# Causal attention stage: per-group helper work moved from ScalarE to VectorE, one multiply folded away, and two look-aheads deepened by one

## The reference

```python
qkv = einsum('bse,fe->bsf', ln(x), w_in)            # 32 query heads, 8 K/V heads, D = 128
q, k = apply_rope(q), apply_rope(k)
scores = einsum('bqhgd,bkhd->bhgqk', q, k) / sqrt(128), causal mask
out = einsum('bhgqk,bkhd->bqhgd', softmax(scores), v)
x = x + ln(einsum('bse,fe->bsf', out, w_out))
xf = ln(x)
routing = softmax(xf @ gate_w.T)                     # 8 experts
y = (xf * (routing @ in_scale)) @ sign(weight).T * (routing @ out_scale) + bias
x = x + ln(y)
```

## Time and profile before

| what | us |
|---|---|
| two timed runs | 9707.69, 9943.1 (median 9825.4) |
| profiled execution, its time | 9640.5 |
| its span on the slowest core (core 4) | 9639.0 |
| spans of all cores | 9559.4 to 9639.0 |
| attention in it (about 2451 to 5883) | 3432 |
| mean granted TensorE clock, all cores | 0.675 to 0.679 |

### The profile page before, as it was taken

How to read it: one execution, slowest core, us unless ns; L and a number is a source line. 1 busy time by engine, 2 the same in 40 slices (tenths; PEclk the granted TensorE clock), 3 DMA queues, 4 the chain that set the end, 5 groups by cost and what they waited for, 6 DMA issues and landing times.

```text
span 9639.0 us, 67201 instructions; the slowest of 8 cores (9559.4 to 9639.0 us)
## 1 busy us (share of the span) xinstructions
PE 6412.1 (67%) x22496; PEld 2183.9 (23%) x22496; DVE 1823.5 (19%) x1540; ACT 1753.5 (18%) x2929; POOL 248.5 (3%) x283
## 2 busy tenths in 40 slices
PE   1277777786567778888888886888831157988400
PEld 1133333333111111111111111333310023333100
DVE  3211111111232111111111110000034450000244
ACT  2200000001333232222222220000012211111111
POOL 0011111100000000000000000000000000000000
PEclk7688888898555555555555555799965569999755
DMA  2221122222100000000000003112122222121233
GB/s 89 72 40 36 37 40 40 40 45 65 42 10 24 6 6 22 5 4 5 4 4 4 4 4 97 41 43 51 46 93 109 109 69 50 34 50 45 78 140 139
DMA packets 118321, 442.99 MB, mean 46 GB/s; under 512 B 13665, under 2 KB 87521, under 8 KB 88033
## 3 DMA queue, kind: packets, MB, share of 16 engines
q0 software_dynamic: 16912, 119.74, 6.9%
q10 hardware_dynamic: 12962, 176.18, 4.7%
q1 hardware_dynamic: 88128, 142.78, 4.1%
HBM read 415.78 MB, written 142.61 MB: 58 GB/s over the span
## 4 chain that ended last, share of the span: by engine, by line
PE 65%; DMA 12%; DVE 12%; ACT 5%; issue 3%; another core or an unknown queue 1%; POOL 1%; ACTq 0%; DVEq 0%; POOLq 0%; SPq 0%
PE PA L544 6%; PE PA L358 5%; PE PB L358 5%; DVE recT_sb L605 4%; DMA wq_sb<-wqkv 4%; PE PB L562 3%; PE PB L572 3%; PE PA L691 3%; PE PB L691 3%; PE PF L537 3%; PE PE L537 3%; PE PB L853 3%; PE PA L853 3%; DVE stats L228 3%; DMA x_t<-xin 3%
## 5 line engine op out<-in xcount | busy, mean ns | idle before, releaser
L605 DVE RECIPROCAL recT_sb<-PA 1x512 f32<-1x512 f32 x128 | 428.2, 3346 | 2110.2 <-PE PA L544 2110.2
L544 PE MATMUL PA<-ptb,ones_bf 128*1 128x512 bf16 (+3 forms) x1280 | 665.6, 520 | 0.0
L608 PE MATMUL PA<-recT_sb,ones_f 1*128 1x512 f32 x256 | 261.3, 1122 | 460.5 <-DVE recT_sb L605 460.5
L358 PE MATMUL PB<-arena,wq_sb 128*128 128x512 bf16 x2048 | 476.6, 396 | 127.0 <-DMA wq_sb<-wqkv 127.0
L358 PE MATMUL PA<-arena,wq_sb 128*128 128x512 bf16 x2048 | 476.7, 396 | 111.7 <-DMA wq_sb<-wqkv 111.7
L594 ACT ACTIVATE ptb<-PB 128x512 bf16<-128x512 f32 (+1 forms) x640 | 333.6, 573 | 626.0 <-PE PB L572 615.4
L562 PE MATMUL PB<-q_sb,k_sb 128*128 128x512 bf16 (+1 forms) x640 | 371.7, 581 | 1.6
L572 PE MATMUL PB<-nmxT_sb,ones_bf 1*128 1x512 bf16 (+1 forms) x640 | 371.8, 581 | 0.0
L691 PE MATMUL PB<-wslot,arena 128*128 128x512 bf16 x1344 | 313.5, 397 | 57.2 <-DMA wslot<-wout 57.2
L853 PE MATMUL PB<-wslot,arena 128*128 128x512 bf16 x1344 | 304.4, 386 | 70.1 <-ACT wslot L823 70.1
L537 PE MATMUL PE<-ptb,vtm 128*128 128x512 bf16 (+3 forms) x640 | 347.2, 542 | 0.0
(11 more groups left out here) (192 smaller groups left out, 6426.3 us busy)
## 6 DMA issues: line engine op xcount, KB each, us to landing
x_t<-xin ACTq DMA_DIRECT2D x32, 2048.0 KB, 9.2
wq_sb<-wqkv POOLq DMA_DIRECT2D x48, 1024.0 KB, 9.1
wslot<-wout POOLq DMA_DIRECT2D x32, 1024.0 KB, 17.0
x2s<-ln2tmp SPq DMA_DIRECT2D x16, 2048.0 KB, 6.3
wslot<-wffn POOLq DMA_DIRECT2D x32, 1024.0 KB, 16.7
x_t<-x2s ACTq DMA_DIRECT2D x16, 2048.0 KB
out<-y_t SPq DMA_DIRECT2D x16, 2048.0 KB, 9.8
Qs<-qout_sb SPq DMA_DIRECT2D x128, 128.0 KB, 7.3
```

The source lines that it names most:

```text
L358: do("tensor", lambda e, p=p, ec=ec, tb=tb, a=sl["ap"]: e.matmul(a[:, :], wq_sb[p][:, ec * 128:(ec + 1) * 128], arena[:, ec * S + tb * 512 ...
L544: e.matmul(sums_ap[0:1, j0 * 128: j0 * 128 + cw], ones_bf1[:, 0:1], ptb[pb][:, j0 * 128: j0 * 128 + cw], start=(kc == 0), stop=(kc == nkc ...
L605: vrc = do("vector", lambda e, sp=sp: e.reciprocal(recT_sb[sp][0:1, :], sums_ap[0:1, 0:512]), inc="sV", waits=(("sT", pe_grp),))
L608: do("tensor", lambda e, sp=sp: e.matmul(sums_ap[:, 0:512], ones_f[:, :], recT_sb[sp][0:1, :], start=True, stop=True), inc="sT", waits=((" ...
```

## The change

Six edits, all in attention:

1. The square of q in `mk_nmx` goes from ScalarE (`activation Square`) to VectorE (`tensor_mul` of bf16 by bf16).
2. The ScalarE multiply by 0.5 is dropped; the factor becomes the `scale` of the Exp.
3. The copy of the spread reciprocals from PSUM to `bcast_sb` goes from ScalarE to VectorE.
4. The waits on those two results change their semaphore accordingly.
5. `pend_pv` may hold three chunks instead of two before `emit_pv` is called.
6. `mk_nmx` runs three groups ahead instead of two.

```diff
-        asq = do("scalar", lambda e, hg_=hg_, qp_=qp_, par=par: e.activation(
-            qsq[par][:, :], q_sb[qp_][:, hg_ * 512:(hg_ + 1) * 512], AF.Square,
-            bias=0.0, scale=1.0),
-            inc="sA", waits=(("sQL%d" % qp_, qhist_g[g]), ("sT", qn_pe[par]),
+        asq = do("vector", lambda e, hg_=hg_, qp_=qp_, par=par: e.tensor_mul(
+            qsq[par][:, :], q_sb[qp_][:, hg_ * 512:(hg_ + 1) * 512],
+            q_sb[qp_][:, hg_ * 512:(hg_ + 1) * 512]),
+            inc="sV", waits=(("sQL%d" % qp_, qhist_g[g]), ("sT", qn_pe[par]),
                              ("sA", KN_A), ("sV", qn_chain[0])))
         do("tensor", lambda e, par=par: e.matmul(
             PA[0:1, 0:512], ones_bf1[:, 0:1], qsq[par][:, :],
             start=True, stop=True), inc="sT",
-           waits=(("sA", asq),))
+           waits=(("sV", asq),))
         qn_pe[par] = cnt("sT")
         aln = do("scalar", lambda e: e.activation(
             nrow_f[0:1, :], PA[0:1, 0:512], AF.Ln, bias=0.0, scale=1.0),
             inc="sA", waits=(("sT", qn_pe[par]),))
-        am = do("scalar", lambda e: e.mul(nrow_f[0:1, :], nrow_f[0:1, :], 0.5),
-                inc="sA", waits=(("sA", aln),))
         ae = do("scalar", lambda e, H=H: e.activation(
             nrow_f[0:1, :], nrow_f[0:1, :], AF.Exp,
-            bias=stats[0:1, 16 + H:17 + H], scale=1.0),
-            inc="sA", waits=(("sA", am),))
+            bias=stats[0:1, 16 + H:17 + H], scale=0.5),
+            inc="sA", waits=(("sA", aln),))
...
-                wpv = wpv + (("sV", pvb["free"]), ("sA", max(bc_last)))
+                wpv = wpv + (("sV", pvb["free"]), ("sV", max(bc_last)))
...
-            while len(pend_pv) > 2:
+            while len(pend_pv) > 3:
                 emit_pv(*pend_pv.pop(0))
...
-        bc = do("scalar", lambda e, sp=sp: CP(e, bcast_sb[sp][:, :],
-                                              sums_ap[:, 0:512]),
-                inc="sA", waits=(("sT", pe_bc), ("sV", bcast_used[sp])))
+        bc = do("vector", lambda e, sp=sp: e.tensor_copy(bcast_sb[sp][:, :],
+                                                         sums_ap[:, 0:512]),
+                inc="sV", waits=(("sT", pe_bc), ("sV", bcast_used[sp])))
         bc_last[g % 2] = bc
-        wev = (("sA", bc),)
+        wev = (("sV", bc),)
...
-            while next_nmx[0] < NG and next_nmx[0] <= g + 2:
+            while next_nmx[0] < NG and next_nmx[0] <= g + 3:
```

## The result

The changed kernel takes 10263.96 us (median of 11 runs, 10171.76 to 10401.32), the kernel before 9745.83 us in the runs made beside it (median of 10). The ratio is **1.061, 95% interval 1.053 to 1.069**: slower, by 6.1%. In some executions the cores of one die, or of both, show a lower granted clock outside attention and the time is some per cent longer: the two medians hold such executions (their quotient alone would be 1.053), the ratio leaves them out. The prediction was 10300 us, within 10080 to 10480.

What follows compares the result with a forecast made beforehand. The prediction took TensorE's in-order list as the bound: 9640.5 + 498 + 122 = 10260 us on the profiled execution, 10328 and 10445 from the lower and median runs. It forecast 10300 us, within 10080 to 10480.

Steps and rivals of the forecast that it cites:

- Part 1: In attention, with three pending, the V matmul waits for the exp of the pair just issued: 384 stalls, 498 us slower.
- Part 2: Between groups, the square waits behind copy and output multiply on VectorE: 0.98 us more at each of 124 borders, 122 us.
- the two bounds: For the bf16 square's time on VectorE, 0.415 and 0.681 us, from rows of other operations; 0.55 was taken.
- Parts 3 and 4: Dropping ScalarE's multiply by 0.5, and preparing the bounds three groups ahead: each predicted to change the time by 0.
- A: Rival: the lagging V matmul waits only for its own exp, leaving just the border's loss, 9762 us; chance 0.07.
- C: Rival: the stalls in attention are half as dear, total about 10000 to 10060 us; chance 0.08.
- D: Rival: each stopped stream in attention also costs 0.3 us of refilling, 115 us more, total 10375 to 10445; chance 0.12.
- B: Rival: the new rhythm of bursts and gaps brings the upper clock in attention, making the kernel faster, 8820 us; chance 0.03.

## Why the prediction was right

*What bounds the kernel.* TensorE's list, as said: every experiment moved attention by what moved in that list, and the 81 us (128 x 0.63) that the folded multiply takes off ScalarE moved nothing by themselves (+0.5 us).

*Part 1, the lag of three.* Predicted 384 stalls and 498 us; measured 384 and 486.2. The single stalls were 1.44, 1.35 and 0.92 against 1.46, 1.35 and 0.92. From these the sum would be 494. The remaining 8 us stand right behind each stall: the V matmul that starts after one is recorded with 0.58 us instead of 0.61, and the sum matmul starts 0.514 us after it, 0.536 where there was no stall (means over the 384 stalls with three pending, and over before's 512 full-width V matmuls behind a score matmul): 384 x 0.022 = 8. So a stopped stream cost nothing on top of the wait; it even gave a little back.

*Part 2, the border.* The mechanism was right and the size was off: 0.80 instead of 0.98 us for each border, 99.3 instead of 122 in all. Four terms were mis-sized. The square of bf16 by bf16 in SBUF takes 0.415 us, the lower of the two bounds, not the middle that I took. It starts 0.08 us before the recorded end of the multiply ahead of it, where I had given it 0.06 after. The wait of one VectorE instruction for another costs 0.17 us, not 0.10, and the copy starts 0.18 us after the spreading matmul's recorded end, not 0.15; these two take a part back. On the square, the Trainium skill, "VectorE: DVE Perf Modes", the section on the perf-mode tiers, gives two elements per cycle for such a multiply; the estimate of 424 ns in the prediction takes that rate and the fixed cost of the page's formula for an fp32 `tensor_tensor`. This trace agrees within 2%, with 415 ns, and I had kept to the middle instead.

What I failed to see was the gain inside this part. I priced the copy and the square together and never asked what each would do alone. A square left on ScalarE runs early, once the copy no longer stands ahead of it there, and the run with the copy alone measured -185 us.

*Parts 3 and 4* at nothing: measured together at +0.5 us, and right for the reason given: in that run the first exps of a group still start 0.15 us after their scores' end, while ScalarE's chain ends 0.8 us ahead of them instead of 0.1 (medians).

*The sum.* 620 us predicted for attention, 586 measured. The profiled execution came out at 10181 us of span where 10260 were expected of it: 34 us are attention, the rest lies in the other stages, which differ by that much between cores anyway (from the end of attention to the end, 3697 to 3756 us before and 3699 to 3707 after). That the number came within 36 us of the measured median is in part luck: it stands on a base of 9680 us (10300 less 620), the median of the wider set of runs of before is 9746, and the error in the base and the 34 us too much in the sum pull in opposite directions. The sum for attention is the part that the runs bear out.

*The rivals.* A is refuted by the 384 waits and by the run in which each V matmul waits for its own exp. C and D, stalls half as dear or dearer by 0.3 us, are refuted by the timelines. B, the clock, did not decide anything, but the sign that I had named for it, a clock above 0.5 in attention, did show: 0.51, from 12 short spells of full clock, 41 us in all on the slowest core. By themselves such signs say little; what counts is what TensorE does in them, see below.

## What to carry to other kernels

A deeper software lag is safe only if what each step waits for is kept as deep as the lag: a record kept for each of the four banks, read when the matmul is emitted, holds a later instruction's count as soon as two pairs have passed, and waiting for a later count leaves the result right and costs only time. An operation moved to an idle engine pays for everything that its new list has ahead of it; ask where in the list it stands, and who ahead of it waits for the path that you want to shorten. When the busiest engine waits at a border, look first at which of its own later work could be written ahead of the wait, and at whether the helper's list lets that help start in time: here this was worth 353 us on top of the 185 that the best move between the engines gave.

## What the runs showed that I had not expected

The granted clock of attention depends on the order in which the same matmuls are issued. The windows over the whole stage (stretch, length, busy times of TensorE, its weight loads, VectorE, ScalarE and GpSimd, PEclk, DMA share, GB/s), first of before on the same stretch as the ruler, then changed, then four pending with their own exps:

```profile
2447.00:5883.00 3436.00, 2787.96 (x6016) 576.30 (x6016) 569.85 (x384) 1004.26 (x1920) 0.00 (x0) 0.50 0.02 9
```

```profile
2453.00:6475.00 4022.00, 2804.19 (x6016) 578.57 (x6016) 702.13 (x640) 780.07 (x1536) 0.00 (x0) 0.51 0.02 7
```

```profile
2449.00:5857.00 3408.00, 2706.86 (x5904) 575.47 (x6016) 569.89 (x384) 1003.92 (x1920) 0.00 (x0) 0.53 0.02 9
```

0.50 before, 0.51 with three pending, 0.53 with four, with the stalls or without them (three pending with their own exps stood at 0.51, four with overwritten counts at 0.53). With two pending it was 0.50 in every run, except in the two whose tail was moved, with 0.51 and 0.52. The number and shapes of the matmuls are the same in all (in the third row 112 matmul records are missing from the trace; the weight loads are all there). So the clock's two levels, 1.2 and 2.4 GHz, answer here to the order of issue.

The trace also says where the upper level comes. With four pending a group of the last three blocks ends with six V matmuls in a row, each with its sum matmul, where it ended with four. Two stretches at such an end (four pending, own exps, core 0), the second over the last matmuls and the wait for the reciprocal:

```profile
4378.50:4381.40 2.90, 2.90 (x7) 0.55 (x6) 0.00 (x0) 0.00 (x0) 0.00 (x0) 0.50 0.00 0
4381.50:4384.50 3.00, 0.79 (x5) 0.35 (x4) 2.10 (x1) 0.00 (x0) 0.00 (x0) 1.00 0.00 0
```

From the last V matmul but one to the last sum matmul, before (core 0) and here:

```profile
4021.64 0.39 PE L537 MATMUL PE<-ptb,vtm 128*128 128x256 bf16 x1
...
4022.48 0.26 PE L544 MATMUL PA<-ptb,ones_bf 128*1 128x128 bf16 x1
```

```profile
4381.50 0.28 PE L538 MATMUL PE<-ptb,vtm 128*128 128x256 bf16 x1
...
4382.08 0.22 PE L545 MATMUL PA<-ptb,ones_bf 128*1 128x128 bf16 x1
```

0.58 us instead of 0.84. On this core the trace has 66 spells of the upper level in attention, 225 us in all, and every one begins 3.7 to 5.0 us ahead of a spreading matmul. TensorE is busy for 29% of them: the last matmuls of the group run faster, and the rest of the spell falls on the wait for the reciprocal, where it is worth nothing. In the groups with such a spell the time from the fourth V matmul from the end to the reciprocal is shorter than the 3.11 us of the others, by 28 to 31 us in all on each core. That is the whole gain of 28.9 us.

The same accounts for the run with four pending and overwritten counts: stalls 351 us, 20 more for the longer first stall of 96 groups, 8 less behind the stalls as in part 1, 26 to 33 less by the clock, depending on the core, together 330 to 337; measured +332. Why that order brings the upper level, and why attention otherwise stays at the lower one, in streams without an idle moment for some 15 us, these runs don't settle.
